# One layer of a perceiver block: order of gating and clip, places of the weight conversions, and one more down product in split form

## The reference

```
x = x + cross_attention(layernorm(x), ctx_512)     # 16 heads of 16; keys and values from a 64-wide context, causal
x = x + self_attention(layernorm(x))               # 16 heads; Wq, Wk, Wv, Wo each with a rank-16 LoRA and a bias
x = x + ffn(layernorm(x))
```

```
logits = flat @ router_w.T
scores = sqrt(softplus(logits))
_, idx = top_k(scores + expert_bias, 4)
topv   = take(scores, idx);  topv = topv / (topv.sum() + 1e-20)
out    = sum over all 32 experts of  p[:, e] * (silu(clip(x @ wg.T)) * clip(x @ wu.T)) @ wd.T   # clip to -7..7, p = 0 if not chosen
```

## Time and profile before

| what | value |
|---|---|
| median of three runs | 73.13 us |
| the profiled execution | 73.51 us, of which the span of the trace is 71.7 us |
| PE matmul busy | 66.4 us (93%) |
| POOL busy | 52.9 us (74%) |
| DVE busy | 46.4 us (65%) |
| ACT busy | 45.6 us (64%) |
| read from HBM | 15.52 MB |

### The profile page before, as it was taken

One profiled execution on the slowest core, in us unless ns is written; L12 is line 12 of the kernel. 1 busy time (PEld: TensorE's weight loads), 2 busy tenths in 40 slices (PEclk: granted clock), 3 DMA queues, 4 the chain that ended last, 5 costly groups with the idle time before them and its releaser, 6 DMA issues.

```text
span 71.7 us, 1577 instructions
## 1 busy us (share of the span) xinstructions
PE 66.4 (93%) x546; PEld 49.4 (69%) x546; DVE 46.4 (65%) x131; ACT 45.6 (64%) x99; POOL 52.9 (74%) x58
## 2 busy tenths in 40 slices
PE   5999997999999999999997999999999999999920
PEld 2347565798864495657775888888888888878910
DVE  0058587684787536798999937635855876698240
ACT  0604556389588656979779999885766974174300
POOL 7311000749999798999896999999999999998000
PEclk9999999999999999999999999999999999999999
DMA  0699999999999999999999995000000000000002
GB/s 0 221 262 287 321 417 418 290 363 412 417 408 406 393 405 333 398 388 381 377 389 397 392 394 204 29 0 0 9 0 0 0 0 0 0 0 0 0 0 73
DMA packets 6342, 15.74 MB, mean 220 GB/s; under 512 B 704, under 2 KB 1472, under 8 KB 6336
## 3 DMA queue, kind: packets, MB, share of 16 engines
q1 hardware_dynamic: 6048, 15.39, 58.6%
q10 hardware_dynamic: 288, 0.27, 1.1%
HBM read 15.52 MB, written 0.13 MB: 218 GB/s over the span
## 4 chain that ended last, share of the span: by engine, by line
PE 70%; DVE 19%; ACT 3%; issue 2%; POOL 1%; DVEq 0%
PE bP L574 16%; PE bY L596 7%; PE bE L437 6%; PE bY L607 6%; PE bXT L586 5%; DVE gu_clip L946 5%; PE bP L374 4%; PE bE L574 4%; PE bY L609 3%; PE bY L426 3%; PE bXT L430 3%; PE bP L401 2%; DVE shifted L842 2%; DVE h L1000 2%; DVE row_max L840 2%
## 5 line engine op out<-in xcount | busy, mean ns | idle before, releaser
L347 POOL TENSOR_TENSOR gu_w<-gu_raw,gu_w 128x512 fp32r<-128x512 f32 x28 | 35.0, 1282 | 1.5 <-ACT gu_w L685 1.3
L574 PE MATMUL bP<-gu_w,xnT_parts 128*128 128x512 f32 x66 | 18.8, 420 | 0.0
L946 DVE TENSOR_SCALAR gu_clip<-bP,clip_at 128x512 f32<-128x512 f32 x13 | 10.4, 805 | 6.4 <-PE bP L574 6.4
L574 PEld LDWEIGHTS bP<-gu_w,xnT_parts 128*128 128x128 f32 x66 | 12.2, 189 | 2.9 <-issue 0.5
L685 ACT ACTIVATE gu_w<-gu_raw 128x1024 fp32r<-128x1024 f32 x10 | 10.5, 1051 | 1.1 <-DMA gu_raw<-moe_w_dram 1.1
L358 POOL TENSOR_TENSOR gu_w<-dn_w,gu_w 128x512 fp32r<-128x512 f32 x7 | 8.8, 1300 | 0.0
L781 ACT ACTIVATE hT_parts<-bXT 128x256 fp32r<-128x256 f32 x10 | 3.8, 384 | 7.3 <-PE bXT L586 7.3
L1000 DVE SCALAR_TENSOR_TENSOR h<-gu_clip,gate,bP 128x128 f32<-128x128 f32 x26 | 7.7, 338 | 0.0
L586 PE MATMUL bXT<-consts_sb,h 128*128 128x128 f32 x33 | 6.3, 274 | 0.5 <-DVE h L1000 0.5
L336 POOL TENSOR_TENSOR aw_sb<-aw_sb,lora_v 128x256 f32<-128x256 f32 x2 | 1.4, 727 | 7.0 <-DMA aw_sb<-attn_w_dram 7.0
L586 PEld LDWEIGHTS bXT<-consts_sb,h 128*128 128x128 f32 x33 | 4.4, 140 | 2.9 <-DVE h L1000 0.9
(11 more groups left out here) (162 smaller groups left out, 124.8 us busy)
## 6 DMA issues: line engine op xcount, KB each, us to landing
gu_raw<-moe_w_dram SPq DMA_DIRECT2D x16, 512.0 KB, 9.7
dn_w<-moe_w_dram SPq DMA_DIRECT2D x16, 256.0 KB, 8.7
aw_sb<-attn_w_dram SPq DMA_DIRECT2D x2, 512.0 KB, 8.3
shared_sb<-shared_w_dram SPq DMA_DIRECT2D x1, 384.0 KB, 15.2
small_sb<-small_dram SPq DMA_DIRECT2D x1, 370.0 KB, 8.2
xwq_sb<-x_wq_dram SPq DMA_DIRECT2D x1, 256.0 KB, 3.8
lora_sb<-lora_dram SPq DMA_DIRECT2D x1, 256.0 KB, 5.6
ctx_sb<-ctx_kv_dram ACTq DMA_DIRECT2D x1, 192.0 KB, 3.5
```

Source lines behind the costliest of these rows:

```text
L347: nc.gpsimd.tensor_tensor(gu_w[:, gu_slot(p), 1, cols], gu_raw[:, raw_slot(p), cols], gu_w[:, gu_slot(p), 0, cols], ALU.subtract).then_inc ...
L574: last = nc.tensor.matmul(bGU[n % 5][:, 0:GU], xnT_parts[:, a, k, :], gu_w[:, gu_slot(n - 1), w, k * GU:(k + 1) * GU], start=(k == 0 and a ...
L946: nc.vector.tensor_scalar(gu_clip[:, n % 4, 0:width], bank[:, 0:width * 2 * I], clip_at[:, 0:1], clip_at[:, 1:2], ALU.min, ALU.max).then_i ...
```

## The change

Five groups of edits:

- DVE, step n of the experts: `gate_h(n)` is now issued ahead of `clip(n + 2)`.
- LAST goes from 10 to 11: pair 6 (p = 5) gets a split down product too.
- POOL: `inverse_sqrt(1)` moves from ahead of the conversions to behind the first half of pair 2's `gu_low`; `inverse_sqrt(2)` moves from the middle of pair 6 to ahead of pair 7. The first four low parts of the down weights are made between those of pairs 12 to 15, the other seven at the end.
- ACT: conversions are made earlier and in other places between the waits. Pair 2 is converted in halves. `dn_high` comes one or two steps earlier.
- PE and DVE: the first half of x's transpose (`add_x_to_xt(0)`) is issued ahead of the first transposition of heads; DVE's `merge_lora(0, 1)` moves ahead of the two `normalise_heads`.

```diff
-EARLY = 9
-LAST = 10
+EARLY = 10
+LAST = 11
+BETWEEN = 12
...
# POOL
-            inverse_sqrt(1)
             pool.wait_ge(bo_mean_ready, 1)
             nc.gpsimd.tensor_scalar(bo_centred[:], ...)
...
-            for p in range(WHOLE, PAIRS):
-                for c in range(DC):
-                    if (p, c) == (WHOLE + 4, 1):
-                        inverse_sqrt(2)
-                    gu_low(p, c)
-            for i in range(LAST):
+            def dn_low(i):
                 pool.wait_ge(dn_hi_ready, i + 1)
...
+            for p in range(WHOLE, PAIRS):
+                for c in range(DC):
+                    if (p, c) == (WHOLE, 1):
+                        inverse_sqrt(1)
+                    if (p, c) == (WHOLE + 5, 0):
+                        inverse_sqrt(2)
+                    gu_low(p, c)
+                if p >= BETWEEN:
+                    dn_low(p - BETWEEN)
+            for i in range(PAIRS - BETWEEN, LAST):
+                dn_low(i)
# PE
             attend(0, 1)
+            pe.wait_ge(lora_merged, 2)
+            add_x_to_xt(0)
             transpose_heads(0, 0)
...
-            pe.wait_ge(lora_merged, 2)
-            add_x_to_xt(0)
             for k in range(DC):
                 add_to_xt(0, k, xwo, 0)
# ACT
-            gu_high(WHOLE)
+            gu_high_chunk(WHOLE, 0)
+            gu_high_chunk(WHOLE, 1)
             gu_high_chunk(WHOLE + 1, 0)
...
             for c in range(DC):
+                gu_high_chunk(WHOLE + 2, c)
                 act.wait_ge(q_psum, DC + c + 1)
...
-            gu_high(WHOLE + 2)
+            gu_high(WHOLE + 3)
             exp_half(1, 0)
...
-            gu_high(WHOLE + 3)
+            gu_high(WHOLE + 4)
...
-            gu_high_chunk(WHOLE + 4, 0)
+            gu_high_chunk(WHOLE + 5, 0)
...
-            gu_high_chunk(WHOLE + 4, 1)
-            gu_high_chunk(WHOLE + 5, 0)
+            gu_high_chunk(WHOLE + 5, 1)
...
-            gu_high_chunk(WHOLE + 5, 1)
-            gu_high_chunk(WHOLE + 6, 0)
+            gu_high(WHOLE + 6)
...
-            gu_high_chunk(WHOLE + 6, 1)
+            gu_high_chunk(WHOLE + 7, 0)
             silu_unit(0)
             silu_unit(1)
-            for p in range(WHOLE + 7, EARLY + 1):
-                gu_high(p)
+            gu_high_chunk(WHOLE + 7, 1)
+            gu_high(EARLY)
+            silu_unit(2)
             hT_unit(0, width=1)
-            silu_unit(2)
             for n in range(1, PAIRS + 1):
...
-                if 0 <= n - 4 < UNITS:
-                    dn_high(n - 4)
+                if 0 <= n - 2 < UNITS:
+                    dn_high(n - 2)
                 for i in range(UNITS, LAST):
-                    if dn_from(i) + 1 == n + 3:
+                    if dn_from(i) + 1 == n + 4:
                         dn_high(i)
# DVE
             merge_lora(0, 0)
+            merge_lora(0, 1)
             normalise_heads(0, 0)
             normalise_heads(0, 1)
-            merge_lora(0, 1)
             merge_lora_whole(1)
...
             for n in range(2, PAIRS + 1):
+                gate_h(n)
                 if n + 2 <= PAIRS:
                     clip(n + 2)
-                gate_h(n)
```

More of the change, by code:

```diff
@@ L438, in keep_busy, with add_x_to_xt @@
                                      start=True, stop=True, skip_group_check=True)
+            def add_x_to_xt(c):
+                nc.tensor.matmul(bXT[c][:, 0:T], x_sb[:, c * 128:(c + 1) * 128], ident, start=True, stop=False,
+                                 skip_group_check=True)
             keep_busy(WARM, bE[:])
@@ L486, in _ @@
             add_to_y(0, 1, xwo).then_inc(y_psum, 1)
-            def add_x_to_xt(c):
-                nc.tensor.matmul(bXT[c][:, 0:T], x_sb[:, c * 128:(c + 1) * 128], ident, start=True, stop=False,
-                                 skip_group_check=True)
-            pe.wait_ge(lora_merged, 2)
-            add_x_to_xt(0)
             for k in range(DC):
@@ L688, in gu_high_chunk @@
                 act.wait_ge(ld_gu[p], 16)
+                if p - WHOLE >= SLOTS:
+                    act.wait_ge(gu_ready, p - SLOTS + 2)
                 cols = slice(c * GU, (c + 1) * GU)
```

## The result

The changed kernel takes 72.16 us in the median (71.80 to 72.35, five runs), the kernel before 73.13 (72.88 to 73.47). The ratio is 0.9847, with a 95% interval of 0.9809 to 0.9885.

What follows compares the result with a forecast made beforehand. PE alone bounds 38.7 to 67.9 us; before that PE, DVE, ACT and POOL take turns. 1.09 - 0.50 - 0.10 - 0.16 = +0.33 gave a median of 73.46 us, range 72.3 to 74.2.

Steps and rivals of the forecast that it cites:

- The second root: Second layernorm: POOL's root waits behind pair 2's first low part and its late weights, so xnT starts later, +1.09 us.
- rival A: Pair 2's raw weights land early: 72.6 us if 0.85 us earlier, 72.37 if 1.3 earlier; chance 0.28.
- The hole at 38 us: PE's wait before pair 2's transpose closes because DVE gates pair 2 ahead of clip(4), -0.50 us.
- hT_low late by 0.10: Near 64 us, hT_low(12) no longer waits behind gate(14), so PE's transpose of pair 14 starts earlier, -0.10 us.
- The eleventh split: Down products on PE: six whole ones become five, a split one taking 0.71 us instead of 0.87, -0.16 us.
- Third root: Third layernorm: POOL's root behind all of pair 6 is still in time for var_eps, 0 us, with 0.6 to spare.
- x's transpose and the LoRA merge: Moved up before the second layernorm on PE and DVE, hidden by PE's longer wait for the root, 0 us.
- ACT's chunks: ACT's earlier conversions of pairs 4 to 7 lie in waits, 0 us, bounds 0 and +0.1.
- POOL's end: POOL finishes its last part at 66.6 us, ahead of the last product's need, with 1.2 us of cover.
- B: Pair 2's raw weights land later than in the trace; 0.8 us later gives 74.3 us; chance 0.12.
- C: PE's hole at 38 us stays since silu(2) is late, pair 10's weights missing: +0.83, 73.96 us; chance 0.05.
- D: PE's clock falls after its stand before 17.2 us, projections take twice as long: 75.5 us; chance 0.05.

Runs made afterwards that it cites:

- roots_back: Changed kernel with both of POOL's inverse_sqrt back at their old places: 72.30 us, ratio 0.9854 to the kernel before.
- after: The changed kernel itself, first trace, against the kernel before: 72.16 us, ratio 0.9847.
- after_again: The changed kernel once more, no edit, on the same chip as roots_back: 72.30 us, ratio 0.9864 to the kernel before.
- root_first: Changed kernel with only inverse_sqrt(1) put back ahead of bo_centred and all conversions: 72.84 us, ratio 0.9922 to the kernel before.
- swap: Changed kernel with SP's loads of pairs 2 and 3 swapped: 72.36 us, from the one execution that counts.

## Why the prediction was wrong, step by step

- *The second root, +1.09.* This step failed. Measured: +0.09 and +0.19 in stage A. The place of the root costs one for one, as I had it, but only from the point at which the first low part overruns var_eps, and with the usual landing that overrun is 0.25 to 0.36, of which the first 0.13 costs nothing (against roots_back, stage A is 0.12 to 0.23 longer). I took the one landing that I had for the kernel's, gave the early landing (rival A) 0.28, and argued its chance from the DMA rate in one window, a rate that is as low when the weights land early. No row of the one trace could have told that its landing was the odd one. Both bounds, 0 and +1.09, stood in my text, and the choice between them rested on one sample.
- *The hole at 38 us, -0.50.* Right place, too small: -0.60 in stage B1 with the gating alone, -0.61 to -0.66 in the one step of PE. I took the idle time of the row. In the stream the transposes start 0.16 before the end of the product ahead, and the stand takes this too.
- *hT_low late by 0.10*: right place, a little small: -0.15 in PE's step. That B2 fell by just 0.11 with the gating alone is a coincidence, since POOL's first down part took 0.09 back.
- *The eleventh split, -0.16*: right, 0.15 in PE's step. With hT_low and what the stand left behind it this makes 0.35 of stage B2, where after and after_again have 0.29 and 0.39.
- *Third root 0*: right, with 0.96 us of POOL's wait before it, but only since the second root had moved; alone it would have cost 0.6 (root_first).
- *x's transpose and the LoRA merge 0*: right. Stage A is 6.68 with them and the roots back (roots_back) and 6.69 to 6.72 without.
- *ACT's chunks 0, bound 0.1*: right in most traces, 0.29 in after_again. I had not counted that a conversion moved ahead of a copy brings its load with it.
- *POOL's end, cover 1.2*: right. It ended at 65.2, and PE asked at about 66.6.

Rival A at its early end (72.37) is what happened; that 72.16 is still below it fits the higher price of the hole and of hT_low. B's landing showed only in an outlying trace, C's condition (pair 10's weights late) did not hold, and D did not come for a stand of 1.45 us in the one trace that has it.

## What to carry to other kernels

When a step that was a pure wait is filled with work that itself depends on a transfer, take the landing from several executions, or work out the cost for each landing: it is a threshold, free below and one for one above. The idle time ahead of a row is not the whole price of a stand on PE: compare the steps from start to start, with and without it. A gain on PE also moves up the moment at which it asks the other engines for something, and can run into the next wait. And on an engine with one queue, two moves can be worth nothing together and cost 0.6 us when only one is made: ask of each what it makes room for.

## What the runs showed of the hardware that was not expected

The first matmuls may run at half pace for far longer than the nine fillers, with the granted clock of the windows at 1.00. The chain of swap, against 1.09 for the same eight in the changed kernel's chain:

```profile
7.53 2.00 PE bP L381 x8
```

```profile
6.53 1.09 PE bP L381 x8
```

The products before these are slow in the same way (1.15 in place of 0.82 for the four of L455), and so the second exponential starts at 12.31 in place of 10.23. And a stand of 2.35 us at 52 us was followed, over a microsecond after PE had resumed, by a granted clock of 0.50, in five of six executions by their means, while one of 1.45 us at 16 us left it at 1.00.
